# A recurrent attention part reordered on all engines: other orders and PSUM banks, three root steps for four, and the inverse's 32 level in two batches

## The reference, cut to what matters

```python
q = silu(causal_dwconv(x @ Wq, qcw, qcb))      # 4 taps
k = silu(causal_dwconv(x @ Wk, kcw, kcb))      # k * 128 ** -0.5
v = silu(causal_dwconv(x @ Wv, vcw, vcb))
alpha, beta = sigmoid(x @ Wa + ba), sigmoid(x @ Wb + bb)
def step(S, inps):
    qt, kt, vt, at, bt = inps
    err = einsum('bhvk,bhk->bhv', S, kt) - vt
    S = at * S - bt * (err[..., None] * kt[:, :, None, :])
    return (S, einsum('bhvk,bhk->bhv', S, qt))
o = (o - mean(o)) * rsqrt(var(o) + 1e-05) * ln_w + ln_b
o = (o * sigmoid(x @ Wg)) @ Wo
```

## Time and profile before

| | us |
|---|---|
| median of 3 runs | 3222.46 (3219.46 to 3222.54) |
| the profiled execution | 3221.71 |
| its span | 3219.9 |
| TensorE busy over the span | 3097.7 (96%) |
| VectorE busy | 2068.3 (64%) |
| ScalarE busy | 1655.6 (51%) |
| GpSimd busy | 1308.0 (41%) |

### The profile page before, as it was taken

How to read it: one execution, slowest core, us unless ns; L and a number is a source line. 1 busy time by engine, 2 the same in 40 slices (tenths; PEclk the granted TensorE clock), 3 DMA queues, 4 the chain that set the end, 5 groups by cost and what they waited for, 6 DMA issues and landing times.

```text
span 3219.9 us, 61611 instructions
## 1 busy us (share of the span) xinstructions
PE 3097.7 (96%) x23984; PEld 2572.4 (80%) x23984; DVE 2068.3 (64%) x3598; ACT 1655.6 (51%) x3880; POOL 1308.0 (41%) x2351
## 2 busy tenths in 40 slices
PE   8999989999999999999999989999999999999999
PEld 6888867887788877877788768778888888888887
DVE  6112267777777777777777733565666666666666
ACT  4221357777777777777777753344333333222222
POOL 2322335555565555555655434422333332222212
PEclk9999999999999999999999989999999999999999
DMA  2100121111111111111111035511000111000004
GB/s 90 30 20 27 67 57 44 38 54 54 38 44 54 54 45 39 53 54 38 47 51 54 28 123 173 150 40 35 28 30 27 30 33 39 27 20 25 25 17 157
DMA packets 130245, 165.71 MB, mean 51 GB/s; under 512 B 9937, under 2 KB 72145, under 8 KB 129921
## 3 DMA queue, kind: packets, MB, share of 16 engines
q1 hardware_dynamic: 120592, 144.49, 15.0%
q10 hardware_dynamic: 9296, 17.04, 1.5%
q0 software_dynamic: 64, 0.23, 0.0%
HBM read 127.91 MB, written 33.82 MB: 50 GB/s over the span
## 4 chain that ended last, share of the span: by engine, by line
PE 75%; DVE 10%; POOL 8%; issue 4%; ACT 2%; DMA 1%; ACTq 0%; SPq 0%; DVEq 0%; POOLq 0%
PE bank L70 21%; PE bank L72 20%; PE bank L71 20%; DVE b_OS L1565 3%; PE bank L938 2%; POOL b_ss L1725 2%; PE bank L1066 2%; PE bank L1092 2%; POOL b_ss L1723 2%; PE bank L1091 2%; PE bank L1076 2%; POOL b_ss L1727 1%; PE bank L1051 1%; DVE b_XPA L1482 1%; DVE b_zt L1459 1%
## 5 line engine op out<-in xcount | busy, mean ns | idle before, releaser
L1459 DVE SCALAR_TENSOR_TENSOR b_zt<-b_rx,b_cw,b_zt 128x512 f32<-128x512 f32 x576 | 484.1, 840 | 39.8 <-ACT b_zt L1215 22.5
L70 PE MATMUL bank<-b_XH,b_wh 128*128 128x512 f32 x1024 | 457.4, 447 | 15.2 <-ACT b_zt L1215 11.0
L71 PE MATMUL bank<-b_XL,b_wh 128*128 128x512 f32 x1024 | 404.4, 395 | 0.7 <-issue 0.7
L72 PE MATMUL bank<-b_XH,b_wl 128*128 128x512 f32 x1024 | 404.4, 395 | 0.0
L70 PE MATMUL bank<-b_XH,b_qh 128*128 128x512 f32 x1024 | 399.3, 390 | 1.4 <-DVE b_g L2573 1.4
L72 PE MATMUL bank<-b_XH,b_ql 128*128 128x512 f32 x1024 | 398.7, 389 | 0.0
L71 PE MATMUL bank<-b_XL,b_qh 128*128 128x512 f32 x1024 | 398.6, 389 | 0.0
L2672 POOL TENSOR_TENSOR b_QHL<-b_qhd,b_QHH 128x512 fp32r<-128x512 f32 x128 | 181.4, 1420 | 477.0 <-ACT b_QHH L2451 474.4
L1703 POOL TENSOR_TENSOR b_PR<-b_A,b_T 128x15 f32<-128x15 f32 (+7 forms) x480 | 169.4, 353 | 200.5 <-issue 164.6
L2451 ACT CAST b_QHH<-b_qhd 128x512 fp32r<-128x512 f32 x128 | 79.5, 622 | 308.3 <-PE bank L72 186.8
L70 PEld LDWEIGHTS bank<-b_XH,b_wh 128*128 128x128 f32 x1024 | 194.5, 190 | 50.5 <-ACT b_zt L1215 13.3
(11 more groups left out here) (249 smaller groups left out, 7654.3 us busy)
## 6 DMA issues: line engine op xcount, KB each, us to landing
b_abc<-tmp_a SPq DMA_DIRECT2D x64, 256.0 KB, 4.0
b_gbc<-tmp_g SPq DMA_DIRECT2D x64, 256.0 KB, 3.5
tmp_og<-b_gg SPq DMA_DIRECT2D x64, 256.0 KB, 2.1
b_mo<-tmp_og SPq DMA_DIRECT2D x64, 256.0 KB, 3.3
b_wr<-in_Wk SPq DMA_DIRECT2D x16, 256.0 KB, 5.3
b_wr<-in_Wq SPq DMA_DIRECT2D x16, 256.0 KB, 5.6
b_wr<-in_Wv SPq DMA_DIRECT2D x16, 256.0 KB, 3.9
b_wr<-in_Wg SPq DMA_DIRECT2D x16, 256.0 KB, 4.3
```

The costliest lines, as they stand in the source:

```text
L70: e.do.matmul(out, wh, xh, start=first and k == 0, stop=False)
L71: e.do.matmul(out, wh, xl, start=False, stop=False)
L72: m = e.do.matmul(out, wl, xh, start=False, stop=last and k == n - 1)
L1459: e.do.scalar_tensor_tensor(out=z[:, :], in0=rx[:, j:j + 512], scalar=cw[:, u // 2, KIND[name[0]], j:j + 1], in1=z[:, :], op0=ALU.mult, op ...
```

## The change

It touches the recurrent part alone. The orders of the steps are rewritten on all engines, and with them the age of the units: q, k1, q1 and v1 are projected for the newest unit, g1 for `i - 2`; `scores` 0 is at the end of the round before the other three. The banks of the small groups are dealt anew. `inverse5` and `inverse6` are cut into three groups (first half of 5; first half of 6 with the second half of 5; second half of 6), and `out5` into two. The root has three steps for four, so that the result is computed with one Newton step less. On SyncE the loads of `decays` stand behind the `store` of b = 0.

```diff
-PROJECTIONS = (("g1", 3), ("q0", 1), ("k1", 1), ("q1", 1), ("v1", 1), ("g0", 2), ("k0", 0), ("v0", 0))
+PROJECTIONS = (("g0", 2), ("k0", 0), ("v0", 0), ("g1", 2), ("q0", 0), ("k1", 0), ("q1", 0), ("v1", 0))
 TURNS = (
-    ("kv0", 2, 2), ("kv1", 2, 1), ("kv2", 2, 0), ("s3", 2, 1), ("s4", 2, 1), ("s5", 2, 0),
-    ("s6", 2, 2), ("sc0", 1, 3), ("s7a", 2, 0), ("s78", 2, 2), ("sc1", 1, 1), ("sc2", 1, 3),
-    ("turn0", 3, 0), ("kv3", 2, 1), ("sc3", 1, 2), ("turn1", 3, 0),
+    ("s7a", 2, 1), ("s78", 2, 3), ("sc1", 1, 2), ("sc2", 1, 1), ("sc3", 1, 2), ("turn0", 3, 0),
+    ("kv3", 2, 3), ("kv0", 1, 0), ("turn1", 3, 2), ("kv1", 1, 3), ("kv2", 1, 0), ("s3", 1, 1),
+    ("s4", 1, 2), ("s5a", 1, 2), ("s56", 1, 1), ("sc0", 0, 0),
 )
...
 SyncE, a round:
+        load_next("v", i - 1)
         products(i - 1, 1)
-        load_next("v", i - 1)
+        store(i - 3, 0)
+        products(i, 0)
+        load_next("g", i - 1)
         decays(i, 0)
-        load_next("g", i - 1)
-        store(i - 3, 0)
         store(i - 3, 1)
         ahead(i - 2, 1)
-        products(i, 0)
         decays(i, 1)
...
 TensorE, the 32 level:
+    def inverse5_first(u):
+        bank_free(e, "s5a", u)
+        e.wait_ge("tmn", u + 1)
+        for m in range(4):
+            r = inverse5(u, m)
+        r.then_inc(S["s5"], 1)
+    def inverse56(u):
+        bank_free(e, "s56", u)
+        e.wait_ge("zt", 2 * u + 1)
+        for m in range(4):
+            inverse6(u, m)
+            r = inverse5(u, m + 4)
+        r.then_inc(S["s5"], 1)
+    def inverse6_second(u):
+        e.wait_ge("zt", 2 * u + 2)
+        for m in range(4, 8):
+            r = inverse6(u, m)
+        r.then_inc(S["s6"], 1)
```

More of the change, by code:

```diff
@@ L1113, in attn0_pe @@
     for i in range(NU + 3):
[L1114 to L1146, removed]
@@ L1147, in attn0_pe @@
-        project(i - 1, "q1", 1, 2)
-        chain1(i - 2, 0)
[L1149 to L1153, removed]
+        chain1(i - 2, 0)
         project(i - 1, "v1", 1, 2)
-        inverse6(i - 2)
+        inverse7_first(i - 2)
+        project(i - 2, "g0", 0, 1)
         project(i - 1, "v1", 2, 3)
-        project(i - 2, "g0", 0, 1)
-        scores(i - 1, 0)
-        inverse7_first(i - 2)
@@ L1181, in attn0_pe @@
+        chain1(i - 2, 2)
+        turn_kv(i - 1, 2)
         project(i, "v0", 1, 2)
-        chain2(i - 2, 1)
+        chain2(i - 2, 2)
         project(i, "v0", 2, 3)
+        project(i - 2, "g1", 1, 2)
+        project(i, "v0", 3, 4)
+        chain4(i - 2, 2)
+        chain3(i - 2, 2)
+        project(i - 2, "g1", 2, 3)
+        project(i, "q0", 0, 1)
+        chain1(i - 2, 3)
+        project(i, "q0", 1, 2)
+        project(i - 2, "g1", 3, 4)
+        ahead(i - 2, 0)
+        ahead(i - 2, 1)
@@ new lines, in attn0_pe @@
+        ahead(i - 2, 2)
+        chain2(i - 2, 3)
+        ahead(i - 2, 3)
+        project(i, "q0", 2, 3)
+        project(i, "k1", 0, 1)
+        project(i, "q0", 3, 4)
+        project(i, "k1", 1, 2)
+        chain4(i - 2, 3)
+        project(i, "k1", 2, 3)
+        project(i, "q1", 0, 1)
+        inverse3(i - 1)
+        project(i, "k1", 3, 4)
+        inverse4(i - 1)
+        project(i, "q1", 1, 2)
+        chain3(i - 2, 3)
+        ahead(i - 2, 4)
+        inverse5_first(i - 1)
+        project(i, "q1", 2, 3)
@@ L1186, in attn0_act @@
+        inverse56(i - 1)
+        project(i, "q1", 3, 4)
+        project(i, "v1", 0, 1)
+        inverse6_second(i - 1)
+        scores(i, 0)
 def attn0_act(e, k, t, mt):
@@ L1386, in attn0_act @@
     for i in range(NU + 3):
+        taken(i - 1, "v0")
+        chain4(i - 3, 2)
+        turned_kv(i - 2, 2)
+        sums(i - 3, 2)
+        finish(i - 1, "k0")
+        gate(i - 3, 1)
+        ahead(i - 3, 3)
+        chain2(i - 3, 3)
+        ahead(i - 3, 4)
+        spread(i - 2, 0)
+        spread(i - 2, 1)
+        taken(i - 1, "q0")
+        chain4(i - 3, 3)
+        sums(i - 3, 3)
+        ahead(i - 3, 5)
+        out3(i - 2)
+        cut_next("k", i - 1)
+        finish(i - 1, "v0")
+        taken(i - 1, "k1")
+        finish(i - 1, "q0")
+        out5(i - 2, 0)
+        lower4(i - 2)
+        out5(i - 2, 1)
         taken(i - 1, "q1")
@@ L1595, in attn0_dve @@
     for i in range(NU + 3):
+        taps(i - 1, "q0")
+        first_guess(i - 3)
+        added4(i - 2)
+        decay(i - 1, 2)
         taps(i - 1, "k1")
-        chain1(i - 2, 0)
+        chain3(i - 3, 3)
+        ahead(i - 3, 4, 6)
         taps(i - 1, "q1")
         scaled(i - 3, 0)
-        scaled(i - 3, 1)
+        chain1(i - 2, 0)
         masked(i - 1, 0)
@@ L1614, in attn0_dve @@
         masked(i - 1, 7)
+        scaled(i - 3, 1)
+        gated(i - 3, 0)
         chain3(i - 2, 0)
@@ L1623, in attn0_dve @@
         chain1(i - 2, 2)
+        taps(i, "k0")
+        gated(i - 3, 1)
+        chain3(i - 2, 2)
         ahead(i - 2, 0, 1)
-        decay(i, 2)
-        taps(i, "k0")
-        chain3(i - 2, 2)
         ahead(i - 2, 1, 2)
@@ L1738, in attn0_pool @@
     for i in range(NU + 3):
+        cut_next("k", i - 1)
         root(i - 3, 0)
+        tail(i - 1, "q0")
+        tail(i - 1, "k1")
+        root(i - 3, 1)
         halo(i - 1, "q1")
-        cut_next("q", i - 1)
[L1742 to L1750, removed]
+        tail(i - 1, "q1")
+        root(i - 3, 2)
+        decayed_q(i - 1, 0)
+        halo(i - 1, "v1")
+        halo(i, "k0")
+        ones(i - 1)
+        decayed_q(i - 1, 1)
+        cut_next("q", i - 1)
+        off_diagonal(i - 1)
         cut_next("v", i - 1)
-        halo(i, "k0")
+        rows(i - 1, 0)
         tail(i - 1, "v1")
-        rows(i - 1, 0)
         rows(i - 1, 2)
```

142 lines of the change are left out of this document (57 added, 85 removed), and 2 rows, old and new, of the table EMPTIED.

## The result

The changed kernel took 3215.38 us in the median of 13 runs (3210.29 to 3220.31), the kernel before 3223.18 us beside it (3219.46 to 3226.55). The ratio is 0.9976, interval 0.9967 to 0.9984: 7.8 us faster. Forecast were 3183 us and a range of 3162 to 3213. The direction was right, the size was a fifth of the forecast, and the time lies outside the range.

The account below looks back on a forecast made before the run. TensorE was taken to set the pace in the first attention layer's recurrent part. Terms summed to 1.25 us a unit, times 30 periods 37.5 us, with the end 39.5: 3222.5 - 39.5 = 3183 us, range 3162 to 3213.

Parts of the forecast that it names:

- The wait of the scores: TensorE's score products (L938) wait for VectorE's masked; the 1.20 us a unit was taken as gone.
- The root step: One GpSimd root step fewer takes 1.1 to 1.8 us off the path root, scaled, masked, sc2.
- Everything else moved: New order on all engines: TensorE stays the bound by 0.9 us; 0.2 us a unit charged for new small waits.
- Issue gaps I leave where they are: TensorE gaps that nothing in the profile releases, 0.6 us a unit, were taken as unchanged.
- The clock: TensorE drops to 1.2 GHz after long waits; 0.25 us a unit taken as regained, bounds 0 and 0.5.
- The batches: The 32 level in two batches: one more entry and exit among TensorE's projections, costing 0.25 us a unit.
- The decay row: SyncE's decays load now stands behind the store; costed at nothing, with 0.7 us of cover.
- rival 3: The decay row lands late, VectorE stalls and TensorE with it: slower, 3248 us; chance 0.09 with its kin.
- The rule weighed: VectorE and GpSimd hold a shared port pair exclusively; speaks against the change, by it the sum would be rival 1's.
- rival 1: The latency loop from inverse3 to the next inverse3 becomes the bound through long holds: about 3209 us; chance 0.17.
- The end: The last turn waits for scaled, which waits for the roots; 2 us gained, bounds -2 and +4.
- Rival 4: The scores' wait only moves, reappearing at inverse3 or inverse5: 3220 us, within 4 us; chance 0.06.

Follow-up runs that it names:

- a_roots4: The changed kernel with four root steps again for three; 3209.14 us, ratio 0.9964 to the kernel before.
- b_roots3: The kernel before with three root steps for four and nothing else; 3192.50 us, ratio 0.9907.
- a_all: The changed kernel with g0's last piece before k0's, inverse4 in two halves, and inverse5 and inverse6 whole; 3172.76 us, ratio 0.9847.
- a_gate_i4: The changed kernel with g0's last piece before k0's, the gate ahead of taken k0, and inverse4 in two halves; 3178.79 us, ratio 0.9859.
- b_fg: The kernel before with VectorE's first_guess ahead of added4 and nothing else; 3196.52 us, ratio 0.9919.
- b_i4_fg: The kernel before with inverse4 in two halves and first_guess ahead of added4; 3194.16 us, ratio 0.9914.
- b_r3_i4: The kernel before with three root steps and inverse4 in two halves, its own orders and banks; 3196.34 us, ratio 0.9918.
- a_kv: a_gate_i4 with the transposes kv 1 ahead of chain2 of chunk 1; 3181.78 us, ratio 0.9874 to the kernel before.
- a_i4: The changed kernel with inverse4 in two halves around a q1 projection piece, later q1 pieces one place down; 3195.57 us, ratio 0.9918 to the kernel before.
- b_i4: The kernel before with inverse4 in two halves around a projection piece and nothing else; 3237.17 us, ratio 1.0045.

## Why the prediction was wrong, step by step

- **The wait of the scores** (-1.20 us a unit) was rightly read and removed in full. Its groups (scores, inverse7 and 8) gained 1.56 us, with the clock behind the wait. The margin of 1.7 us at sc3 agrees with a_roots4, where one step more (1.1 to 1.8 us) brings no wait back.
- **The root step**, 1.1 to 1.8 us and most of the wait by itself: right, b_roots3 takes the wait from 34.6 to 11.5 us and the time down by 30.
- **"Everything else moved"** is the step that failed, and in it the walk through the new order. It charged 0.2 us a unit for new waits, and the sum even added 0.25 for small waits that would leave, most of it the gate's 3.8 us in 20 units. The gate's wait did not leave, it rose to 9.2 us in 20 units. The walk named three thin margins, inverse4, inverse5 and inverse3, and none was this one: nowhere does it ask what each wait counts. The shared counter made `taken` k0 start at g0's end, 1.6 us after k0's, and the gate and v0 came behind it. Cost: 0.7 us a unit in chain3 with the wait behind it; undoing it gave 24 us.
- **"Issue gaps I leave where they are"**: the second step that failed. They rose by 11 us (21.2 to 32.6), 0.4 us a unit, and spreading one group gave 20 us with the clock. Why the new order lengthens them is not shown. Both orders have five projection pieces between inverse3 and the end of inverse6. One difference that the traces show: before, in 15 of 31 units, `chain1` stood with one piece between inverse3 and inverse4; now one piece stands there alone, and inverse4 starts 1.58 us after inverse3 in the median, for 1.80.
- **The clock** (-0.25 us a unit): not regained. The two kernels spend 23.9 us each at 1.2 GHz between 470 and 1800 us. Before, it fell seven times, each time at a wait of the scores; now three times, at the three longest instruction gaps.
- **The batches** (+0.25 us a unit): 0.1 to 0.2 by a_all against a_gate_i4, at the edge of what these runs can tell.
- **The decay row** (rival 3): right to cost it at nothing. VectorE waited 7.5 us for it in 20 units (6.5 before), and TensorE shows no wait behind it.
- **The rule weighed** (rival 1's long holds): the decay scans took 0.42 us in the median and 1.17 at most, for 0.41 and 1.49 before, so no longer holds came with the new order.
- **The end** (-2 us): the last turn came 6 us earlier (1909.99 us for 1916.15). The second layer's first products start 4 us earlier (2172.5 for 2176.5), so 2 us were given back in between.

So the forecast's 1.25 us a unit became 0.01: the gain came as read, and new waits and gaps of the same size ate it. Rival 4 came nearest: the wait went away and others of the same total took its place, at the gate and at instruction blocks instead of inverse3 or inverse5. Its chance of 0.06 was too low. The latency loop (rival 1) was not the bound: TensorE, freed twice, ran at 44.2 us a unit.

Left open: the 0.4 to 0.75 us a unit that the projections cost more than before in every variant of the new order. The order can't be the whole reason, since in the old order too they go from 24.49 us to between 24.77 and 24.96 once the scores wait less (b_fg, b_roots3, b_i4_fg, b_r3_i4). Waits of chain2 for R are 0.1 us a unit of it, and moving one group (a_kv) did not lower the total. Not run were three root steps together with `first_guess` ahead of `added4`, which in the old order might remove what is left of the scores' wait.

## What to carry to other kernels

When two tasks share a counting semaphore, their order on the producer is part of every wait on it. If the list and the producer disagree, whichever task ends first counts as the first on the list: one wait ends late, and the other would end too early. Look at what stands in front of the critical step in its queue before rewriting the queues: here two exchanged lines gave 26 us and one dropped step 30, where the whole change, with that step and a new order on all engines, gave 8. And where many small matmuls stand together, spread them among long ones, unless the step behind them is on the critical path (a_i4 gained 20 us, b_i4 lost 14 by the same edit).

## What the runs showed of the hardware

- TensorE can run out of instructions. The trace has one 16 KB transfer for each 256 of its records, and all 48 gaps in the 32x32 groups, before and after, stand at a boundary of 256 records. The transfer ahead of a gap started 2.2 to 2.9 us before work went on and took 0.9 to 1.5 us itself. A gap cost up to 2.4 us. The profile shows this as "issue". Among projections and other full-size products, 6 records in 0.7 us, only 3 of 124 boundaries show a gap over 0.4 us.
- Such a gap can take the clock with it: the 1.73 us gap at 770 us was followed by 6.8 us at 1.2 GHz, and the two of 2.2 us, near 819 and 1277 us, went with 10.2 and 6.8. With the small products spread, in the profile of a_i4, the clock did not fall once between 470 and 1800 us.
